# A graph network, mixer and expert layer: accumulations that follow the products by two steps, and one-hot turns through a single PSUM bank

## The reference, cut to what matters

```python
h = (x @ W).reshape(n, HEADS, OUT_C)            # 8 heads x 32
a1 = jnp.sum(h * attn_l, axis=-1)
a2 = jnp.sum(h * attn_r, axis=-1)
e = jax.nn.leaky_relu(a1[src] + a2[dst], negative_slope=NEG_SLOPE)
ex = jnp.exp(e - seg_max[dst])
denom = jax.ops.segment_sum(ex, dst, num_segments=n)
out = jax.ops.segment_sum(h[src] * (ex / denom[dst])[:, :, None], dst, num_segments=n)
...
x = x + gnn(xn) + mix(xn)
x = x + ffn(layernorm(x))
```

## Time and profile before

| what | us |
|---|---|
| median of 3 runs | 3325.59 |
| lowest and highest | 3318.01, 3342.11 |
| time of the profiled execution | 3324.99 |
| its span (first to last instruction) | 3323.2 |

### The profile page before, as it was taken

How to read it: one execution, slowest core, us unless ns; L and a number is a source line. 1 busy time by engine, 2 the same in 40 slices (tenths; PEclk the granted TensorE clock), 3 DMA queues, 4 the chain that set the end, 5 groups by cost and what they waited for, 6 DMA issues and landing times.

```text
span 3323.2 us, 49035 instructions
## 1 busy us (share of the span) xinstructions
PE 2365.4 (71%) x13450; PEld 1740.1 (52%) x13451; DVE 1661.5 (50%) x3416; ACT 614.6 (18%) x1640; POOL 1894.6 (57%) x1764
## 2 busy tenths in 40 slices
PE   4767767666766676666667666777877775489997
PEld 2545555444544555445455455555655554347776
DVE  6444545444544545445445545555555554733334
ACT  2411111111111111111111111111111111143332
POOL 3366666666666666666666766666666667200000
PEclk8777878788878788878878887888889887789999
DMA  6633333333333333333333333333333333100000
GB/s 195 204 84 98 97 96 94 94 91 97 92 95 93 95 95 99 92 95 93 95 95 95 97 91 103 102 107 104 109 107 106 108 92 90 30 28 20 19 19 20
DMA packets 150659, 302.18 MB, mean 91 GB/s; under 512 B 36164, under 2 KB 88348, under 8 KB 150621
## 3 DMA queue, kind: packets, MB, share of 16 engines
q0 software_dynamic: 82848, 233.35, 26.4%
q1 hardware_dynamic: 66100, 66.77, 6.2%
q10 hardware_dynamic: 1672, 1.59, 0.2%
HBM read 269.29 MB, written 32.29 MB: 91 GB/s over the span
## 4 chain that ended last, share of the span: by engine, by line
PE 44%; another core or an unknown queue 24%; issue 14%; DVE 13%; ACT 3%; DVEq 2%; ACTq 0%; DMA 0%; SPq 0%; POOL 0%; POOLq 0%
PE bank L873 18%; PE bank L986 5%; PE bank L837 4%; PE bank L976 4%; PE bank L825 3%; DVE acc L1272 3%; DVE work L1265 3%; PE bank L882 3%; PE bank L880 2%; PE bank L891 1%; PE bank L786 1%; PE bank L925 1%; DVE zb L1248 1%; DVE zb L1246 1%
## 5 line engine op out<-in xcount | busy, mean ns | idle before, releaser
L549 POOL DMA_INDIRECT work<-h_tab,idx x1712 | 1851.3, 1081 | 874.1 <-issue 458.6
L873 PE MATMUL bank<-work 128*128 128x264 f32 x3424 | 1074.1, 465 | 445.5 <-DVE work L1265 218.4
L873 PEld LDWEIGHTS bank<-work 128*128 128x128 f32 x3424 | 740.3, 229 | 619.2 <-issue 426.3
L1272 DVE TENSOR_TENSOR acc<-bank,acc 128x264 f32 x856 | 369.0, 431 | 775.0 <-PE bank L873 326.6
L1265 DVE TENSOR_TENSOR work<-work 128x1024 f32<-128x1024 f32 x428 | 506.3, 1224 | 44.3 <-issue 36.6
L648 ACT CAST work<-bank 128x512 bf16<-128x512 f32 x428 | 236.8, 588 | 784.9 <-remote 365.2
L837 PE MATMUL bank<-a2p,work 128*128 x5136 | 245.6, 173 | 154.0 <-ACT work L648 97.4
L837 PEld LDWEIGHTS bank<-a2p,work 128*128 128x128 bf16 x5136 | 220.3, 99 | 235.8 <-issue 195.1
L654 ACT ACTIVATE work<-zb 128x64 f32<-128x64 f32 x214 | 54.9, 256 | 1435.9 <-DVE zb L1250 1137.5
L825 PE MATMUL bank<-ident,work 128*128 128x128 f32 x1712 | 267.5, 301 | 28.6 <-issue 27.9
L1246 DVE TENSOR_TENSOR zb<-work,bank 128x64 f32<-128x64 f32 x214 | 46.8, 219 | 482.0 <-remote 448.6
(11 more groups left out here) (236 smaller groups left out, 1811.2 us busy)
## 6 DMA issues: line engine op xcount, KB each, us to landing
work<-h_tab,idx POOLq DMA_INDIRECT x1712
xx_d<-acc SPq DMA_DIRECT2D x49, 256.0 KB, 2.1
xnt_c<-xx_d SPq DMA_DIRECT2D x66, 128.0 KB
h_tab<-acc SPq DMA_DIRECT2D x49, 132.0 KB, 1.9
xn_c<-xx_d SPq DMA_DIRECT2D x49, 128.0 KB
q2t_d<-q2t_c SPq DMA_DIRECT2D x49, 128.0 KB
X<-x SPq DMA_DIRECT2D x6, 1024.0 KB, 11.7
out<-wqkv SPq DMA_DIRECT2D x16, 384.0 KB, 2.6
```

The lines of the kernel that those rows point to most:

```text
L549: nc.gpsimd.indirect_dma_start(out=ring[q][:, j, :], out_offset=None, in_=h_tab, in_offset=bass.IndirectOffsetOnAxis(ap=idx[:, q, j:j + 1] ...
L873: ins = mm(bank[3 + s % 2][:, 0:TW], hot[q][:, s * G + g, :], ring[q][:, s * G + g, :], start=(g == 0), stop=(g == G - 1))
L1272: v.tensor_tensor(a, bank[3 + s % 2][:, 0:TW], a, ALU.add).then_inc(added, 1)
```

## The change

VectorE's additions go two steps (LAG = 2) behind: in batch b it adds steps 2 and 3 of batch b-1 and steps 0 and 1 of batch b. The new order on DVE is: product 0, add of step 2 of b-1, product 1, add of step 3 of b-1, one-hots of b+2, [mix additions], add 0, exponents of b+1, add 1, [q and k scaled]. The last two additions follow the loop. On PE the two halves of `turned` are split: half 0 stays ahead of step 0, half 1 goes behind step 0, both write bank 0, and each waits for the cast of the half before it; `pick` goes from ahead of step 2 to right behind step 1, and no longer waits for product 1. ACT reads bank 0 for both halves. The products and the one-hots keep their operands in SBUF. The waits of the steps for `added` keep their counts. The numbers of instructions of the loop stay as they are.

```diff
@@ ScalarE
                     act.wait_ge(hot_turned, b * 2 + k + 1)
                     nc.scalar.copy(hotT[q][:, k * 4:k * 4 + 4, :].rearrange("p j d -> p (j d)"),
-                                   bank[k][:]).then_inc(hotT_kept, 1)
+                                   bank[0][:]).then_inc(hotT_kept, 1)
@@ TensorE
-            def turned(b, q):
-
-                pe.wait_ge(hot_ready, b + 1)
-                for k in range(2):
-                    wait(pe, hotT_kept, b * 2 + k - 1)
-                    for j in range(4):
-                        ins = turn(bank[k][:, j * P:(j + 1) * P], hot[q][:, k * 4 + j, :], ident[:])
-                    ins.then_inc(hot_turned, 1)
+            def turned(b, q, k):
+
+                if k == 0:
+                    pe.wait_ge(hot_ready, b + 1)
+                wait(pe, hotT_kept, b * 2 + k)
+                for j in range(4):
+                    ins = turn(bank[0][:, j * P:(j + 1) * P], hot[q][:, k * 4 + j, :], ident[:])
+                ins.then_inc(hot_turned, 1)
...
                 if not last:
-                    turned(b + 1, (q + 1) % R3)
+                    turned(b + 1, (q + 1) % R3, 0)
                 for s in range(SB):
                     if s % 2 == 0:
                         pe.wait_ge(msg_ready, b * 2 + s // 2 + 1)
-                    if s == 2 and not last:
-                        pick(b + 1, (q + 1) % R3)
                     wait(pe, added, b * SB + s - 1)
...
                     ins.then_inc(summed, 1)
+                    if s == 0 and not last:
+                        turned(b + 1, (q + 1) % R3, 1)
+                    if s == 1 and not last:
+                        pick(b + 1, (q + 1) % R3)
@@ VectorE
+                    n = b * SB + s
+                    dve.wait_ge(summed, n + 1)
+                    wait(dve, added, n)
+                    a = acc[:, bass.ds(ts[s + before], TW)]
                     v.tensor_tensor(a, bank[3 + s % 2][:, 0:TW], a, ALU.add).then_inc(added, 1)
...
+                dve.wait_ge(ex_ready, b + 1)
+                scale(0)
+                if not begin:
+                    add(-2)
+                scale(1)
+                if not begin:
+                    add(-1)
+                if not last:
+                    one_hots(b + 2, (q + 2) % R3)
                 if side == "mix" and first and q == 0:
...
                 add(0)
                 if not last:
-                    one_hots(b + 2, (q + 2) % R3)
+                    exponents(b + 1, (q + 1) % R3, i + 1 if q < 2 else i + 2)
                 add(1)
-                if not last:
-                    exponents(b + 1, (q + 1) % R3, i + 1 if q < 2 else i + 2)
-                add(2)
                 if side == "qk" and q == 2:
...
-                add(3)
...
+            for n in range(NB * SB - LAG, NB * SB):
+                dve.wait_ge(summed, n + 1)
+                dve.wait_ge(added, n)
+                t = dve.value_load(t_acc[0:1, n:n + 1], min_val=0, max_val=(NT - 1) * TW)
+                a = acc[:, bass.ds(t, TW)]
+                v.tensor_tensor(a, bank[3 + n % 2][:, 0:TW], a, ALU.add).then_inc(added, 1)
```

More of the change, by code:

```diff
@@ L41 @@
 SB = 4
+LAG = 2
 TB = SB * G
@@ L841, in _ @@
             pe.wait_ge(h_kept, NT)
-            turned(0, 0)
+            turned(0, 0, 0)
+            turned(0, 0, 1)
             pe.wait_ge(wvo_kept, 1)
@@ L1256, in batch, with scale @@
                 last = isinstance(i, int) and i == IT
+                begin = isinstance(i, int) and i == 0 and q == 0
+                before = 0 if begin else LAG
                 _, ts = nc.values_load_multi_w_load_instructions(
-                    t_acc[0:1, bass.ds(b * SB, SB)], engines=[mybir.EngineType.DVE], min_val=0,
+                    t_acc[0:1, bass.ds(b * SB - before, before + SB - LAG)], engines=[mybir.EngineType.DVE], min_val=0,
                     max_val=(NT - 1) * TW, skip_runtime_bounds_check_because="steps' node tiles are clamped")
-                dve.wait_ge(ex_ready, b + 1)
-                for k in range(2):
+                def scale(k):
                     m = ring[q][:, k * 4:k * 4 + 4, 0:C].rearrange("p j (h c) -> p j h c", h=H)
@@ L1267, in add @@
                 def add(s):
-                    dve.wait_ge(summed, b * SB + s + 1)
-                    wait(dve, added, b * SB + s)
-                    a = acc[:, bass.ds(ts[s], TW)]
+                    n = b * SB + s
+                    dve.wait_ge(summed, n + 1)
+                    wait(dve, added, n)
+                    a = acc[:, bass.ds(ts[s + before], TW)]
                     v.tensor_tensor(a, bank[3 + s % 2][:, 0:TW], a, ALU.add).then_inc(added, 1)
+                dve.wait_ge(ex_ready, b + 1)
[7 more added lines that the diff above has]
+                    one_hots(b + 2, (q + 2) % R3)
                 if side == "mix" and first and q == 0:
```

## The result

| | before | changed |
|---|---|---|
| median of the runs, us | 3332.68 (3318.01 to 3342.11, 4 runs) | 3748.64 (3746.76 to 3758.21, 4 runs) |
| profiled execution, us | 3324.99, span 3323.2 | 3747.85, span 3746.0 |
| edge loop: window, TensorE busy, clock | 2723 us, 1893.90, 0.82 | 3120 us, 2315.59, 0.73 |
| exponents: "remote" waits | 448.6 us in 93 | 1098.5 us in 197 |
| TensorE's steps waiting for additions | 30.5 us in 23 | 764.1 us in 218 |

The ratio is 1.1258 (95% interval 1.1207 to 1.131). The prediction was 3405 us, range 3230 to 3500: the direction is right, the size is not.

A forecast was written before the change was run, and what follows sets the result against it. It took a cycle of waits through TensorE, VectorE and ScalarE as the bound, with POOL held back by it. Late batches 36 + on-time 54 - low clock 15 + bank 5 = +80 on 3324.99: 3405 us, range 3230 to 3500.

The forecast's parts named there:

- The dependency: Step 3 needs addition 1, now behind the exponents: steps' waits for additions rise to 0.5 us and more a batch.
- The working of an on-time batch: High-clock batch: with mix side work the cycle goes from 8.68 to 9.9 us, without from 7.48 to 7.75.
- the sum (+54 - 15 + 5): Terms besides lateness: on-time batches at high clock +54 us, low clock -15, the turns' single bank +5.
- the late term: Batches whose exponents start late: 66 us in the mix stretch, 43 in qk, 109 together; a third, 36, was taken.
- in-time term: Batches without late exponents lose 1.2 or 0.4 us each: 85 us if the clock is high, 54 taken.
- Rival 3: Much slower: lateness is a given and the casts' lateness comes out, +109 + 54 + 60, 3530 us; chance 0.08.
- The clock: At low clock TensorE's longer steps cover VectorE's extra operations: gain at most 0.45 us in batches without side work, -15 us.
- a rival of +95 at 0.75: More, shorter TensorE pauses move the loop's clock from 0.82: +95 us at 0.75, -110 at 0.90; no separate chance.
- The bank: Both half turns through one bank: half 1 waits for half 0's cast, hidden when posts are in time; 5 us.
- The gathers: Gathers beside one-hot or product rows take 2.01 us; these rows stay in number and kind, so price zero.
- Rival 2: Same: unexplained waits end where POOL has filled its slots and pauses, so only their length changes; +10, 3335 us; chance 0.26.
- rival 1: Faster: product 0 no longer waits for TensorE's steps 2 and 3; -120, 3205 us; chance 0.26.

The follow-up runs named there:

- two_gathers: The changed kernel with GpSimd gathering only two of each batch's eight groups from the fourth batch on: 2620.45 us, 0.7894 of the kernel before.
- TensorE's part alone: The kernel before with only TensorE's and ScalarE's part of the change, VectorE in the old order: 3394.76 us, 1.0191 (3330 chip); 2979.73 us (2970 chip).
- VectorE's order alone: The kernel before with only VectorE's new order of additions, TensorE's part as before: 3522.83 us, 1.0563 (3330 chip); 2939.35 us (2970 chip).

## Why the prediction was wrong

**What bounds the kernel.** Right for this chip: a cycle of waits, with POOL behind it (591.5 and 389.4 us of waits). That POOL's floor of 11.05 us a batch lies below was read from a trace in which TensorE's posts are late. On the 2970 chips the floor is the bound (10.8 us a batch in the changed kernel).

**The dependency.** Right, and the core of the result: step 3 needs addition 1, which now stands behind the exponents. I said 0.5 us a batch and more; 764.1 / 214 = 3.6 us. TensorE's waits for products, 218 us, are gone, as said.

**The working of an on-time batch.** It can be checked where nothing else limits, in `two_gathers`: from step 0 to step 0 the mean of the batches without side work is 8.10 us (median 7.96) against 7.75 worked out, and with mix side work the median is 9.52 (mean 10.19) against 9.9. So the prices were right within 0.4 us, at the high clock that the batch was taken from. But as a forecast of the on-time case the sum (+54 - 15 + 5) has the wrong sign: the 2970 chip gave -42 us, since POOL is what the loop waits for there, and these terms are of engines that have time to spare.

**The step that failed** is the late term: "I take a third, 36, as the mean late wait (4.8) is close to what PE ran ahead by". Three things in it were wrong. First, the lateness is neither a given amount nor a backlog that pauses use up. The pause ahead of step 3 does end it, batch by batch (step 3's post is on time), but the next pick makes it anew. TensorE now pauses 3.5 us a batch (764.1 in 218), and the exponents are late in 197 of 214 batches instead of 93. I had held the number at 93 and asked only how much of it would show. Second, once late, it shows in full, for a long pause ahead of step 3 comes with the low clock. Third, I gave late qk batches side work behind them in one of three cases, the first batch of a group, and took the third batch at 0.4 to 0.5 us. It has side work behind step 3 as well (L891 to L897 before, L895 to L901 now), and it lost most. By the mean periods from step 0 to step 0:

| batches | before, us | changed, us | loss, us | loss in all, us |
|---|---|---|---|---|
| first of a qk group (49) | 14.39 | 16.28 | 1.9 | 92 |
| second (49) | 11.36 | 11.35 | 0.0 | 0 |
| third (49) | 13.07 | 16.77 | 3.7 | 181 |
| mix stretch (49) | 12.64 | 15.48 | 2.8 | 139 |
| the other 17 | | | | 12 |

Together 424 us. That batches with side work lose and those without almost nothing is what the working said (2.1 and 0.1); the number of the first kind was wrong. In the third batches the pick's post comes a median of 5.4 us behind its record, in the first and second 2.2, as in the fences above. Even with all 98 mix and first qk batches late at full price, 49 x 2.1 + 49 x 2.5 = 225, and 25 of the in-time term left for the others, the sum 3324.99 + 225 + 25 - 15 + 5 is some 3565 us, over 180 short. Rival 3 counted only the 48 late ones; its terms add up to 3548 and not 3530 (31 x 2.1 is 65, too, and not 66, which changes nothing).

**The clock** was a term of -15 and a rival of +95 at 0.75. It came out at 0.73. Steps took 1205.7 us in place of 1074.1, and each side multiplication of the first qk batches (L886, before L882) a mean of 1062 ns in place of 724:

```profile
L873 PE MATMUL bank<-work 128*128 128x264 f32 x3424 | 1205.7, 485 | 775.0 <-DVE acc L1279 764.1
```

It was priced by the mean of the loop, but it falls where the pause is: 191 of the 214 steps 3 took over 1.8 us, and of steps 1 and 2 together four. By itself it is no cause: with three banks, so without the coupling, the clock of the whole span is 0.852 in place of 0.765, with the exponents as late. The Trainium skill (TensorE: Matmul & The Clock Gate, The HAM clock gate) says that the throttled clock is the default and activity releases it. The traces agree: 2.13 us at 0.50 for the step behind a pause of 2.84, 1.16 us at 1.00 for the one behind 0.99.

**The bank.** Taken at 5 us. TensorE's waits at the pick for the cast were 97.4 us and are 4.5 now. TensorE's part alone costs 1.9%, some 62 us, on the 3330 chip; on the 2970 chip 8 us by one execution of each. How much of the 62 is the bank and how much the pick's place stays open.

**The gathers.** Priced at zero. On a 2970 chip VectorE's order alone shortened the gathers from 1866.0 us (TensorE's part alone, so VectorE as before) to 1821.6, and the time from 2979.73 to 2939.35. I read that as the slot between the two products; it was not tried by itself, and each time is of one execution. In the trace of TensorE's part alone a gather that starts beside an addition (PSUM and SBUF in) takes 0.94 to 0.96 us, one that overlaps a product or the one-hots (two SBUF inputs) a mean of 1.29 and up to 2.0; with VectorE's order that mean is 1.20. The Trainium skill (SBUF — State Buffer, Who interferes with whom) says that a VectorE instruction with two SBUF inputs contends with GpSimd's reads and that one with a single SBUF input, outside the 2-port modes, does not; these durations agree. That this is the gain of the change where POOL is waited for is likely, not shown.

**The rivals.** Rival 2 (same) and rival 1 (faster) are ruled out as forecasts for this chip. But what rival 2 said of the waits, that they end where POOL has filled its slots and pauses, has something to it. Of the 199 late posts of the pick that can be placed in the changed kernel, 191 come within GpSimd's last gather ahead of a pause or within the pause, which together are 46% of the loop's time. In the first fence the post at 1421.13 comes in the gather from 1420.62, the last of four; in the second, at 1434.94, behind the last of eight. Where two gathers are still to start when the pick's records end, the post is a median of 2.24 us late (145 batches), where three are, 5.39 (37), and where none is, 0.01 (20). The repeat on another chip says the same (2.24, 5.40 and 0.01). In the kernel before the link is not so clean, and POOL itself pauses for late posts of the steps, so which makes which is not shown. What is left open: why TensorE's posts come late on some chips and not on others, and whether its work or only its posts are late. The Trainium skill (Perfetto Trace Analysis, Summary: the profiler window per engine type) says that the end of a TensorE record is estimated and that the semaphore's way is not in it.

## What to carry to other kernels

Before an operation is moved behind a wait, ask how late that wait is in the worst trace, and suppose that its lateness comes in every batch: a moved addition cost 12.6% where it stood behind a wait that was unexplained in 93 of 214 batches, and 1.2% when it stood ahead of it. Then list every batch that has work behind the step that waits, not only the longest kind. A large "remote" share on a single core can mean, as here, that the order's worth depends on the chip: measure on more than one. A third PSUM bank took back 313 of the 420 us that the change lost. Merging many tiny multiplications took the changed order from 1.125 to 0.986 of the kernel before where posts were late; in the order of before it cost 1.6% there, and where posts were on time it changed less than 1% in either order, so it is worth trying only where an engine waits behind them.

## What the runs showed of the hardware

- The kernel before takes 2970 us on some chips and 3330 on others; in the changed kernel TensorE's records of step 1 and the pick have the same lengths on both. What differs is when TensorE's posts arrive: at the pick 0.01 us behind the record's end on the one, a median of 2.25 us on the other.
- In the changed kernel the lateness begins at the pick and ends with TensorE's pause: the posts of step 1, the pick, step 2 and step 3 come a median of 0.01, 2.25, 2.70 and 0.01 us behind their records.
- It needs the full stream of gathers or GpSimd's work on it: with a quarter of the gathers it is gone on a chip that otherwise has it, and that kernel runs in 2620 us.
- With a pick of 8 multiplications in place of 24 the exponents of the changed order wait 253 to 300 us for late posts in place of 1078 to 1098. The casts wait 478 to 609 in place of 37 to 40, so a part of the lateness only moves.
- Gathers take 0.95 us beside an addition and up to 2.0 beside a VectorE operation with two SBUF inputs.
- Two changes that cost 5.6% and 1.9% alone cost 12.5% together.
